# Reordered stages of a fused attention and expert kernel: adjacent cross values, ScalarE prototype norm

## The chip, the core and the metric

The kernel runs on one core of one Trainium2 chip. The metric is device time in microseconds (us) of one execution; lower is better. Runs of one kernel differ by about 0.1% here (1447.82 to 1450.38 us in three).

## What is computed

Four sequences of 1024 rows of 256 numbers, all in fp32, go through two layers. Layer 0 does layer norm, self-attention in windows of 128 rows (16 heads of 16, shifted by 64 rows), top-16 cross-attention to 77 context rows, and a SwiGLU of width 1024, each with a modulation from a condition vector. Layer 1 attends to the same 77 rows as prototypes, routes over three experts, and gates the result. Cut to what matters here:

```
scores = einsum('bqhd,bkhd->bhqk', q, k) / sqrt(D)          # cross-attention, 77 keys
top_s, top_i = top_k(scores, 16);  attn = softmax(top_s)
o = einsum('bhqk,bhqkd->bqhd', attn, take(v, top_i))         # "cross values"
x = x + gate * (o @ w_co + b_co);  x = x + swiglu(ln(x))
nx = layer_norm(x) * gamma + beta                            # layer 1
weights = softmax(nx @ Wq @ (P @ Wk).T / 16);  evidence = weights @ (P @ Wv)
probs = softmax(concat(nx, evidence, anchor) @ router_W + b)
out = x + gate(...) * (sum_e probs_e * expert_e(...) @ out_w + out_b)
```

## The kernel before

The 4096 rows are worked off in 16 units of 256 rows (two tiles of 128), software-pipelined by hand: step k of the function `both` does the self-attention stage for unit a = k + 1, the cross-attention stage for unit c = k, and the MLP and expert stage for unit b = k - 1. After a prologue come 14 steps of `both` (k = 1 to 14), one of `last_cross` (no unit a is left) and one of `last_experts` (unit 15 alone). Each engine has its own copy of these functions with its own order of calls written out, and each engine works strictly in that order. Nothing reorders them at run time; semaphores make one engine wait for another.

All eight PSUM banks are shared by jobs in a fixed order, `BANK_JOBS`. A job's producer on TensorE waits until the previous job of that bank is drained (`wait_free`), and signals `full`; the reader signals `drained`. For the prediction these rows of the table matter: bank 1 holds the self-attention values "v" and then "y01" (turned cross weights of the first tile); bank 2 holds "y02" and then "h00"; bank 4 "mo", then "ln4", then "ps"; bank 5 "m1", "m6", "h01", "h20"; bank 6 "m2", "h10", "e0", "e1"; bank 7 "m7", "wt", "h11", "h21".

The part of a step around the change runs like this:

- TensorE ends the projections of unit a with `a_v` (L826), turns the normalised rows of unit b (`b_turn_normed`, a `turn` of "ln4", four transposes at L776 that read `xnB`), turns the picked cross weights of the first tile (`a_turn_picked(0, s)`, ten transposes at L923 and L930), and multiplies by the prototypes' matrix (`b_proto_scores`, L988, which reads `nxT`). Then come products of the experts' first layer (`b_first_nx`, L1011, eight matmuls each), the turned prototype weights (`b_turn_weights`, L996), the cross values of the first tile (`a_cross_values`, L944 and L950), the evidence products (`b_first_evidence`, L1018), the picked weights of the second tile, the turned inverses of the kept sums (`a_turn_inverses`, L883, reads `kept`), the router (L1003), the cross values of the second tile, and the self-attention scores of unit a (`a_scores`, L844).
- ScalarE copies the values out of bank 1 (`a_copy_values`, writes `va`, L1454), scales the turned rows into `nxT` (`b_affine`, through `modulate`, L1414), copies the turned picks into `probT` (`a_copy_picked`, L1478), takes the exponentials of the prototype scores (`b_proto_exp`, L1554, writes `pw`), then of the second tile's cross scores (`a_cross_exp`, L1499), then copies the turned weights out (`b_copy_weights`, L1560).
- VectorE does the layer norm statistics (`ln_stats`) and their use (`ln_apply`, L2220, writes `xnB`), the top-16 search (`a_topk`, MAX8 and MATCH_REPLACE8 at L2304, L2309 and L2316, the bulk of its work), masks the picked weights (`a_pick`), takes the prototype maxima (`b_proto_shift`, L2351), and normalises the prototype weights (`b_proto_norm`: reciprocal L2357, multiply L2359). The search of the second tile is wrapped around these two. At its end come the kept sums (`a_sum_kept`) and their inverse (`a_invert_kept`, L2285).
- GpSimd computes the inverse deviations (`rstd_of`, L1820 and L1822), subtracts row maxima (`a_shift`, L1835), and spreads the kept inverses (`a_spread`, L1856).

SyncE issues the DMAs (rows of x, results, weights per sequence); the change touches none of them.

Of the kernel before, what the change touches and what calls it, by code (L numbers as in the profile page):

```python
# [147 lines left out]
def bass_pixart_experts(nc, x, cond, ctx_in, w_ada, b_ada, w_qkv, b_qkv, w_so, b_so, w_q, b_q, w_kv, b_kv,  # L148
# [6 lines left out]
    with ExitStack() as stack:  # L155
# [81 lines left out]
        probT = sb("probT", [P, SLOTS, HPS, P])  # L237
        rsum = sb("rsum", [P, TILES, H])
# [350 lines left out]
        def _(pe):  # L589
# [343 lines left out]
            def a_cross_values(t, u):  # L933
# [5 lines left out]
                for e in range(PAR):  # L939
                    wait_drained(pe, f"y{t}{e}", u)  # L940
                    for f, name in enumerate(("xv", "xw")):
                        r = slice(f * MAIN, (f + 1) * MAIN)
                        for s in range(SLOTS):
                            pe.matmul(bank_of(name)[32 * s:32 * s + 32, t * P:(t + 1) * P], vc_main[r, s, 32 * e:32 * e + 32],  # L944
                                      probT[r, e, s, :], start=(e == 0), stop=False, skip_group_check=True)
                wait_drained(pe, f"y{t}2", u)
                for f, name in enumerate(("xv", "xw")):
                    r = slice(f * MAIN, (f + 1) * MAIN)
                    for s in range(SLOTS):
                        last[name] = pe.matmul(bank_of(name)[32 * s:32 * s + 32, t * P:(t + 1) * P], vc_tail[r, s // 2, s % 2, :],  # L950
                                               probT[r, 2, s // 2, :], start=False, stop=True, skip_group_check=True)
# [224 lines left out]
            def both(k, r, batch):  # L1176
# [46 lines left out]
                b_turn_normed(b)  # L1223
# [4 lines left out]
                a_turn_picked(0, 2, c)  # L1228
                if r == 1:
                    pe.wait_ge(readB, batch * 5 + 5)  # L1230
                a_turn_picked(0, 3, c)
                b_proto_scores(b)
                b_first_nx("h00", 0, b)
                b_first_nx("h01", 2 * P, b)
# [4 lines left out]
                if r == 0:  # L1239
                    pe.wait_ge(values_read, batch + 1)  # L1240
                a_cross_values(0, c)
# [7 lines left out]
                b_first_evidence("h10", RH, b)  # L1249
                a_turn_inverses("r2", "xv", c)  # L1250
                b_router(b)
# [38 lines left out]
            def last_cross(c, b):  # L1290
# [21 lines left out]
                b_turn_normed(b)  # L1312
                a_turn_picked(0, 2, c)
                a_turn_picked(0, 3, c)
                b_proto_scores(b)
                b_first_nx("h00", 0, b)
                b_first_nx("h01", 2 * P, b)
                a_cross_values(0, c)
                b_turn_weights(b)
                b_first_nx("h10", RH, b)  # L1320
                b_first_evidence("h00", 0, b)
                b_first_nx("h11", RH + 2 * P, b)
                b_first_evidence("h01", 2 * P, b)
# [4 lines left out]
                b_first_evidence("h10", RH, b)  # L1328
                a_turn_inverses("r2", "xv", c)
                a_cross_values(1, c)  # L1330
                b_first_evidence("h11", RH + 2 * P, b)
                b_router(b)
                a_project("xv", oT2, "co", Wco_g, c)
                b_second(0, (0, 1), b)
                b_first_nx("h20", 2 * RH, b)
                b_second(0, (2, 3), b)
                b_second(1, (0, 1), b)
                b_first_nx("h21", 2 * RH + 2 * P, b)
# [5 lines left out]
                turn("ln3", xnB, c, normed[2], TILES)  # L1344


            def last_experts(b):
# [31 lines left out]
                b_first_evidence("h11", RH + 2 * P, b)  # L1379
                b_second(0, (0, 1), b)  # L1380
                b_first_nx("h20", 2 * RH, b)
                b_second(0, (2, 3), b)
                b_second(1, (0, 1), b)
                b_first_nx("h21", 2 * RH + 2 * P, b)
# [20 lines left out]
        def _(act):  # L1405
# [67 lines left out]
            def a_copy_picked(t, i, u):  # L1473
# [4 lines left out]
                act.activation(probT[:, i, 0:n, :], bank_of(name)[:, 0:n * P].rearrange("p (i q) -> p i q", i=n), ACT.Copy)\  # L1478
# [70 lines left out]
            def b_proto_exp(u):  # L1549
# [6 lines left out]
                i.then_inc(drained[JOB["ps"][0]], 1)  # L1556

# [99 lines left out]
            def both(k, r, batch):  # L1657
# [32 lines left out]
                a_cross_exp(1, 0, c)  # L1690
                b_copy_weights(b)
# [40 lines left out]
            def last_cross(c, b):  # L1732
# [22 lines left out]
                a_copy_picked(0, 2, c)  # L1755
                b_proto_exp(b)
                a_cross_exp(1, 0, c)
                b_copy_weights(b)
                a_cross_exp(1, 1, c)
                a_kept_exp(0, c)  # L1760
# [9 lines left out]
                b_tanh_first("h11", hE[:, 1], 2, 6, b)  # L1770
                b_tanh_first("h20", hE[:, 0], 0, 8, b)
                b_tanh_first("h21", hE[:, 0], 2, 10, b)
                b_tanh_first("hg", gs, 0, 12, b)
                b_modulate(c)

            def last_experts(b):
# [11 lines left out]
                b_proto_exp(b)  # L1788
                b_copy_weights(b)
# [25 lines left out]
        def _(pool):  # L1815
# [146 lines left out]
            def both(k, r, batch):  # L1962
# [11 lines left out]
                a_shift(0, 0, c)  # L1974
                rstd_of(0, EPS0, a)
                wait_full(pool, "ln2", a - 1)
                ln_apply(0, xa, xnA, a)
                a_shift(0, 1, c)
# [22 lines left out]
            def last_cross(c, b):  # L2001
# [14 lines left out]
                a_spread("xv", c)  # L2016
                b_mix_biases(b)
                rstd_of(2, EPS0, c)
# [33 lines left out]
        def _(dve):  # L2052
# [213 lines left out]
            def a_normalise(name, dst, u):  # L2266
# [3 lines left out]
                if name == "xv":  # L2270
                    wait_full(dve, "xw", u)
                    for f, half in enumerate(("xv", "xw")):
# [82 lines left out]
            def b_proto_norm(u):  # L2355
                wait_drained(dve, "ps", u)
                dve.reciprocal(psu[:, :], psu[:, :]).then_inc(proto_steps, 1)  # L2357
                dve.wait_ge(proto_steps, u * 2 + 1)
                dve.tensor_tensor(pw[:, :, :], pw[:, :, :], psu[:, :].rearrange("p (t a) -> p t a", a=1).to_broadcast([P, TILES, LC]),  # L2359
                                  ALU.mult).then_inc(proto_steps, 1)  # L2360
# [168 lines left out]
            def both(k, r, batch):  # L2529

                a, c, b = k + 1, k, k - 1
                ra, xa, xc, xb = (r + 1) % UNITS, xs[(r + 1) % UNITS], xs[r], xs[r - 1]
                b_swiglu(0, b)
# [7 lines left out]
                a_load(ra, batch)  # L2541
                ln_stats(0, xa, a)
# [29 lines left out]
                if r == 1:  # L2572
                    prep_b_evidence(batch, 3, psum[6])
                a_residual(xb, xb, "mo", b)
                wait_drained(dve, "mo", b)
                ln_stats(3, xb, b)
                a_pick(0, 1, c)
# [6 lines left out]
                b_proto_norm(b)  # L2584
# [46 lines left out]
            def last_cross(c, b):  # L2631
# [19 lines left out]
                a_topk("a", 1, 0, c)  # L2651
# [3 lines left out]
                a_pick(0, 1, c)  # L2655
                ln_apply(3, xb, xnB, b)
                a_topk("a", 1, 1, c)
                a_topk("b", 1, 0, c)
                a_topk("a", 1, 2, c)
                b_proto_shift(b)  # L2660
                a_topk("b", 1, 1, c)
                b_proto_norm(b)
# [96 lines left out]
```

## Time and profile before

| | |
|---|---|
| median of 3 runs | 1449.21 us (1447.82 to 1450.38) |
| profiled execution, its own time | 1443.77 us |
| its span, first to last instruction | 1442.0 us |
| instructions | 31061 |
| busy share of the span: TensorE matmul, weight load | 97%, 81% |
| busy share: VectorE, ScalarE, GpSimd | 73%, 58%, 33% |
| mean granted TensorE clock | 0.994 of 2.4 GHz |
| bytes moved | 35 MB, 24 GB/s on average |

The span is measured on the one profiled execution. "Busy" of TensorE counts from the start of a matmul to its modelled end; matmuls overlap, so that the distance between the starts of two neighbours (0.216 us for 256 columns, 0.109 us for a transpose of 128) is what a matmul costs in a stream, not its own length of 0.38 us.

### The profile page before, as it was taken

To read this page: it belongs to the slowest core of one execution; us is meant where nothing else is said; L and a number is where in the kernel's file an instruction comes from. 1 tells how busy PE (TensorE), PEld (TensorE's weight loads), DVE (VectorE), ACT (ScalarE), POOL (GpSimd) and SP (SyncE) were. 2 spreads that over 40 slices of the span, in tenths; PEclk is the share of its full clock that TensorE was granted. 3 is DMA by queue.
4 is the path that set the end of the run, shared out by engine and by line. 5 is a ranking of instruction groups with operands and counts; after the bars stand their busy time and mean duration, and the time that the engine had idled before them with its cause. 6 is when DMAs were issued, how large, how long until landed. Compare 5 with 4: busy or idle time off the path is not lost.

```text
span 1442.0 us, 31061 instructions
## 1 busy us (share of the span) xinstructions
PE 1399.3 (97%) x10145; PEld 1172.1 (81%) x10145; DVE 1050.5 (73%) x4822; ACT 833.3 (58%) x2599; POOL 481.7 (33%) x627
## 2 busy tenths in 40 slices
PE   7989999999999999999999999999999999998997
PEld 5778788888888788888888788888888878887886
DVE  3586869687786868778696786869687786968532
ACT  2473575757566375756647375665757457574423
POOL 1315133333325234332335233233335313332302
PEclk9999999999999999999999999999999999999999
DMA  7510000000010000010010000010010000000000
GB/s 245 202 67 2 1 15 12 9 27 9 19 31 16 1 2 25 2 34 9 19 31 2 15 2 16 11 34 1 9 49 2 16 1 9 1 1 8 2 4 11
DMA packets 27346, 35.06 MB, mean 24 GB/s; under 512 B 3324, under 2 KB 22448, under 8 KB 26929
## 3 DMA queue, kind: packets, MB, share of 16 engines
q1 hardware_dynamic: 27185, 33.07, 7.2%
q8 instruction: 82, 1.34, 0.4%
q14 instruction: 79, 0.65, 0.1%
HBM read 28.83 MB, written 4.22 MB: 23 GB/s over the span
## 4 chain that ended last, share of the span: by engine, by line
PE 80%; DVE 14%; ACT 3%; issue 3%; POOL 1%; SPq 0%; DMA 0%; DVEq 0%; POOLq 0%; ACTq 0%
PE bank L966 12%; PE bank L1011 12%; PE bank L1035 11%; PE bank L1018 6%; PE bank L805 6%; PE bank L975 6%; PE bank L791 5%; DVE knocked L2316 4%; PE bank L854 3%; PE bank L844 2%; PE bank L866 2%; PE bank L923 2%; PE bank L762 2%; PE bank L776 2%; DVE M L2309 2%
## 5 line engine op out<-in xcount | busy, mean ns | idle before, releaser
L966 PE MATMUL bank<-hB,Wm 128*128 128x256 f32 x1024 | 244.3, 385 | 2.2 <-ACT hB L1414 2.2
L966 PEld LDWEIGHTS bank<-hB,Wm 128*128 128x128 f32 x1024 | 191.8, 191 | 33.8 <-issue 7.5
L1011 PE MATMUL bank<-nxT,W1nx 128*128 128x256 f32 x896 | 214.1, 385 | 3.0 <-ACT probT L1478 2.7
L1463 ACT ACTIVATE prob<-bank,rmax 128x128 f32<-128x128 f32 x512 | 179.1, 402 | 29.3 <-DVE rmax L2238 29.3
L1011 PEld LDWEIGHTS bank<-nxT,W1nx 128*128 128x128 f32 x896 | 167.1, 192 | 28.2 <-ACT probT L1478 5.1
L1035 PE MATMUL bank<-W2p,gT 128*128 128x256 f32 x768 | 183.2, 382 | 3.0 <-DVE acc L2395 1.9
L1835 POOL TENSOR_TENSOR scores<-scores,M 128x308 f32<-128x308 f32 x128 | 93.3, 729 | 277.1 <-DVE knocked L2316 275.9
L1035 PEld LDWEIGHTS bank<-W2p,gT 128*128 128x128 f32 x768 | 141.4, 190 | 23.6 <-issue 2.8
L1516 ACT ACTIVATE tbs<-bank,b1half 128x256 f32<-128x256 f32 x128 | 60.5, 473 | 146.4 <-PE bank L966 106.9
L1532 ACT ACTIVATE tbs<-bank,betaH 128x256 f32<-128x256 f32 x224 | 96.3, 497 | 78.4 <-PE bank L1018 78.4
L1820 POOL TENSOR_SCALAR vare<-mv 128x2 f32<-128x2 f32 x64 | 24.9, 388 | 311.8 <-DVE mv L2214 310.5
L1463 ACT ACTIVATION_READ_ACCUMULATOR prob<-bank,rmax 128x1 f32 x512 | 124.2, 243 | 0.0
L975 PE MATMUL bank<-Wm_g,gT 128*128 128x256 f32 x480 | 116.1, 381 | 0.0
L1018 PE MATMUL bank<-wT,Vp 77*128 77x256 f32 x448 | 113.2, 386 | 0.0
L2316 DVE MATCH_REPLACE8 knocked<-M,scores 128x77 f32<-128x77 f32 x512 | 108.4, 223 | 0.2 <-issue 0.2
L2316 DVE MATCH_REPLACE8 knocked<-M,knocked 128x77 f32<-128x77 f32 x512 | 108.3, 222 | 0.2
L975 PEld LDWEIGHTS bank<-Wm_g,gT 128*128 128x128 f32 x480 | 90.3, 190 | 17.0 <-issue 4.2
L2238 DVE TENSOR_REDUCE rmax<-bank 128x4 f32<-128x512 f32 x128 | 80.7, 684 | 21.6 <-PE bank L844 21.6
L1018 PEld LDWEIGHTS bank<-wT,Vp 77*128 77x128 f32 x448 | 80.4, 190 | 14.3 <-issue 5.7
L2304 DVE MAX8 M<-scores 128x8 f32<-128x77 f32 x512 | 83.6, 224 | 0.2
L2309 DVE MAX8 M<-knocked 128x8 f32<-128x77 f32 x512 | 83.1, 223 | 0.0
L2336 DVE SCALAR_TENSOR_TENSOR gT<-tbs,gT 128x256 f32<-128x256 f32 x120 | 51.3, 428 | 37.4 <-ACT gT L1518 37.4
(258 smaller groups left out, 2841.1 us busy)
## 6 DMA issues: line engine op xcount, KB each, us to landing
Wm_g<-in_L_xcond_w_m_dram SPq DMA_DIRECT2D x4, 1024.0 KB, 5.5
W1ev<-in_L_xcond_e_w_dram SPq DMA_DIRECT2D x6, 512.0 KB, 7.3
x<-in_x_dram SPq DMA_DIRECT2D x16, 128.0 KB, 2.4
x<-in_x_dram SPq DMA_DIRECT2D x32, 64.0 KB, 2.3
Wm<-in_L_xcond_w_m_dram SPq DMA_DIRECT2D x1, 2048.0 KB, 8.8
out_dram<-acc SPq DMA_DIRECT2D x16, 128.0 KB, 1.7
out_dram<-acc SPq DMA_DIRECT2D x32, 64.0 KB, 2.0
batch_rows<-row_store SPq DMA_DIRECT2D x4, 384.0 KB, 3.8
```

The source lines that it names most:

```text
L805: m = pe.matmul(bk[:, t * C:(t + 1) * C], src[:, k, t * P:(t + 1) * P], w[:, k, :], start=(opens and k == 0 and t == 0), stop=(k == nk - 1 ...
L966: m = pe.matmul(bank_of(name)[:, half * UT:(half + 1) * UT], Wm1[:, k, c:c + P], hB[:, k, :], start=(k == 0), stop=(k == CB - 1))
L975: m = pe.matmul(bank_of("mo")[:, t * C:(t + 1) * C], gated_of(u)[:, j, t * P:(t + 1) * P], Wm2_g[:, j, :], start=(j == 0 and t == 0), stop ...
L1011: pe.matmul(bank_of(name)[:, n * UT:(n + 1) * UT], W1nx[:, k, c0 + n * P:c0 + (n + 1) * P], nxT[:, k, :], start=(n == 0 and k == 0), stop= ...
L1018: m = pe.matmul(bank_of(name)[:, n * UT:(n + 1) * UT], Vp[:, c0 + n * P:c0 + (n + 1) * P], wT[:, :], start=False, stop=True, skip_group_ch ...
L1035: m = pe.matmul(bank_of(name)[:, t * C:(t + 1) * C], hE[:, e % 2, k, t * P:(t + 1) * P], W2p[:, e * RB + k, :], start=(k == 0 and t == 0), ...
L1463: m = act.activation(prob[:, s, i, :], psum[s][:, i * P:(i + 1) * P], ACT.Exp, bias=rmax[:, t, s * HPS + i:s * HPS + i + 1], accum_out=rsu ...
L1532: act.activation(tb[tb_of(name)][:, n * UT:(n + 1) * UT], bank_of(name)[:, n * UT:(n + 1) * UT], ACT.Tanh, bias=betaH[:, n0 + n:n0 + n + 1 ...
L1835: pool.tensor_tensor(Dx[:, t, g, :], S[:, t, g, :], M12[:, t, g, 0:1].to_broadcast([P, HPS, LC]), ALU.subtract)\
L2304: dve.max(M12[:, t, h, 0:8], S[:, t, h, :]).then_inc(topk, 1)
L2309: dve.max(M12[:, t, h, 8:TOPK], K[:, h, :]).then_inc(topk, 1)
L2316: dve.match_replace(K[:, h, :], top, src, KNOCKED).then_inc(topk, 1)
```

## The change

The turned weights of the first cross tile are copied into `prob` instead of `probT` (`turned_picks`), so that both tiles' turned weights can stand at once, and the two calls of `a_cross_values` follow each other behind `a_turn_inverses`. On TensorE, `b_turn_normed` moves behind all four `a_turn_picked(0, s)`, so that it stands directly ahead of `b_proto_scores`; the products "h01" and "h00" swap; the router moves ahead of the turned inverses. The multiplication of the prototype weights by their inverse sums moves from VectorE (one instruction) to ScalarE (two), behind `a_cross_exp(1, 0)`; only the reciprocal stays on VectorE. VectorE takes the statistics of unit a ahead of `b_swiglu(0)`, and `a_pick(0, 1)` ahead of the MLP's residual. GpSimd does `rstd_of(0)` and `ln_apply(0)` ahead of `a_shift(0, 0)`. In `last_cross` and `last_experts` several blocks change places. The diff, with unchanged lines left out and indentation reduced:

```diff
@@ -235,6 +235,7 @@ buffers
 probT = sb("probT", [P, SLOTS, HPS, P])
+turned_picks = [prob, probT]
 rsum = sb("rsum", [P, TILES, H])
@@ -942,13 +943,13 @@ TensorE, a_cross_values
         pe.matmul(bank_of(name)[32 * s:32 * s + 32, t * P:(t + 1) * P], vc_main[r, s, 32 * e:32 * e + 32],
-        probT[r, e, s, :], start=(e == 0), stop=False, skip_group_check=True)
+        turned_picks[t][r, e, s, :], start=(e == 0), stop=False, skip_group_check=True)
     wait_drained(pe, f"y{t}2", u)
...
         last[name] = pe.matmul(bank_of(name)[32 * s:32 * s + 32, t * P:(t + 1) * P], vc_tail[r, s // 2, s % 2, :],
-        probT[r, 2, s // 2, :], start=False, stop=True, skip_group_check=True)
+        turned_picks[t][r, 2, s // 2, :], start=False, stop=True, skip_group_check=True)
     if t == TILES - 1:
@@ -1220,25 +1221,22 @@ TensorE, both (a = k + 1, c = k, b = k - 1)
     a_v(1, a)
-    b_turn_normed(b)
     if r == 1:
...
     a_turn_picked(0, 2, c)
+    a_turn_picked(0, 3, c)
+    b_turn_normed(b)
     if r == 1:
         pe.wait_ge(readB, batch * 5 + 5)
-    a_turn_picked(0, 3, c)
     b_proto_scores(b)
+    b_first_nx("h01", 2 * P, b)
     b_first_nx("h00", 0, b)
-    b_first_nx("h01", 2 * P, b)
     b_turn_weights(b)
...
     b_first_nx("h10", RH, b)
-    if r == 0:
-        pe.wait_ge(values_read, batch + 1)
-    a_cross_values(0, c)
     b_first_evidence("h00", 0, b)
@@ -1247,8 +1245,11 @@ TensorE, both
     b_first_evidence("h10", RH, b)
+    b_router(b)
     a_turn_inverses("r2", "xv", c)
-    b_router(b)
+    if r == 0:
+        pe.wait_ge(values_read, batch + 1)
+    a_cross_values(0, c)
     a_cross_values(1, c)
@@ -1309,40 +1310,39 @@ TensorE, last_cross
     a_turn_picked(0, 1, c)
-    b_turn_normed(b)
     a_turn_picked(0, 2, c)
     a_turn_picked(0, 3, c)
+    b_turn_normed(b)
     b_proto_scores(b)
+    b_first_nx("h01", 2 * P, b)
     b_first_nx("h00", 0, b)
-    b_first_nx("h01", 2 * P, b)
-    a_cross_values(0, c)
     b_turn_weights(b)
...
     b_first_evidence("h00", 0, b)
+    b_first_evidence("h01", 2 * P, b)
     b_first_nx("h11", RH + 2 * P, b)
-    b_first_evidence("h01", 2 * P, b)
     a_turn_picked(1, 0, c)
...
     b_first_evidence("h10", RH, b)
+    b_router(b)
     a_turn_inverses("r2", "xv", c)
+    a_cross_values(0, c)
     a_cross_values(1, c)
     b_first_evidence("h11", RH + 2 * P, b)
-    b_router(b)
+    b_second(0, (0, 1), b)
     a_project("xv", oT2, "co", Wco_g, c)
-    b_second(0, (0, 1), b)
     b_first_nx("h20", 2 * RH, b)
     b_second(0, (2, 3), b)
+    b_first_nx("h21", 2 * RH + 2 * P, b)
     b_second(1, (0, 1), b)
-    b_first_nx("h21", 2 * RH + 2 * P, b)
+    turn("ln3", xnB, c, normed[2], TILES)
     b_second(1, (2, 3), b)
...
     b_first_evidence("hg", 3 * RH, b)
-    turn("ln3", xnB, c, normed[2], TILES)
-
@@ -1377,11 +1377,11 @@ TensorE, last_experts
     b_first_evidence("h11", RH + 2 * P, b)
+    b_first_nx("h20", 2 * RH, b)
     b_second(0, (0, 1), b)
-    b_first_nx("h20", 2 * RH, b)
     b_second(0, (2, 3), b)
+    b_first_nx("h21", 2 * RH + 2 * P, b)
     b_second(1, (0, 1), b)
-    b_first_nx("h21", 2 * RH + 2 * P, b)
     b_second(1, (2, 3), b)
@@ -1475,7 +1475,7 @@ ScalarE, a_copy_picked
     wait_full(act, name, u)
-    act.activation(probT[:, i, 0:n, :], bank_of(name)[:, 0:n * P].rearrange("p (i q) -> p i q", i=n), ACT.Copy)\
+    act.activation(turned_picks[t][:, i, 0:n, :], bank_of(name)[:, 0:n * P].rearrange("p (i q) -> p i q", i=n), ACT.Copy)\
        .then_inc(drained[JOB[name][0]], 1)
@@ -1554,6 +1554,12 @@ ScalarE, new function
     i.then_inc(drained[JOB["ps"][0]], 1)
+
+def b_proto_norm(u):
+    act.wait_ge(proto_steps, u * 2 + 1)
+    for t in range(TILES):
+        i = act.activation(pw[:, t, :], pw[:, t, :], ACT.Copy, scale=psu[:, t:t + 1])
+    i.then_inc(proto_steps, 1)
@@ -1688,6 +1694,7 @@ ScalarE, both
     a_cross_exp(1, 0, c)
+    b_proto_norm(b)
     b_copy_weights(b)
@@ -1753,11 +1760,12 @@ ScalarE, last_cross
     a_copy_picked(0, 2, c)
+    a_kept_exp(0, c)
     b_proto_exp(b)
     a_cross_exp(1, 0, c)
+    b_proto_norm(b)
     b_copy_weights(b)
     a_cross_exp(1, 1, c)
-    a_kept_exp(0, c)
     b_tanh_first("h00", hE[:, 0], 0, 0, b)
@@ -1768,10 +1776,10 @@ ScalarE, last_cross
     b_tanh_first("h11", hE[:, 1], 2, 6, b)
+    b_modulate(c)
     b_tanh_first("h20", hE[:, 0], 0, 8, b)
...
     b_tanh_first("hg", gs, 0, 12, b)
-    b_modulate(c)
@@ -1786,6 +1794,7 @@ ScalarE, last_experts
     b_proto_exp(b)
+    b_proto_norm(b)
     b_copy_weights(b)
@@ -1971,10 +1980,10 @@ GpSimd, both
     add_bias(1, xc, c)
-    a_shift(0, 0, c)
     rstd_of(0, EPS0, a)
...
     ln_apply(0, xa, xnA, a)
+    a_shift(0, 0, c)
     a_shift(0, 1, c)
@@ -2014,8 +2023,8 @@ GpSimd, last_cross
     a_spread("xv", c)
+    rstd_of(2, EPS0, c)
     b_mix_biases(b)
-    rstd_of(2, EPS0, c)
@@ -2269,7 +2278,7 @@ VectorE, a_normalise
         wait_full(dve, "xw", u)
-        for f, half in enumerate(("xv", "xw")):
+        for f, half in ((1, "xw"), (0, "xv")):
         dve.tensor_tensor(dst[:, f, :], bank_of(half)[:, 0:UT], oT2[:, f, :], ALU.mult).then_inc(drained[JOB[half][0]], 1)
@@ -2352,12 +2361,9 @@ VectorE, b_proto_norm
-def b_proto_norm(u):
+def b_proto_invert(u):
     wait_drained(dve, "ps", u)
     dve.reciprocal(psu[:, :], psu[:, :]).then_inc(proto_steps, 1)
-    dve.wait_ge(proto_steps, u * 2 + 1)
-    dve.tensor_tensor(pw[:, :, :], pw[:, :, :], psu[:, :].rearrange("p (t a) -> p t a", a=1).to_broadcast([P, TILES, LC]),
-        ALU.mult).then_inc(proto_steps, 1)
@@ -2530,6 +2536,8 @@ VectorE, both
     ra, xa, xc, xb = (r + 1) % UNITS, xs[(r + 1) % UNITS], xs[r], xs[r - 1]
+    a_load(ra, batch)
+    ln_stats(0, xa, a)
     b_swiglu(0, b)
@@ -2538,8 +2546,6 @@ VectorE, both
         prep_m(batch)
-    a_load(ra, batch)
-    ln_stats(0, xa, a)
     a_topk("a", 0, 1, c)
@@ -2571,17 +2577,17 @@ VectorE, both
         prep_b_evidence(batch, 3, psum[6])
+    a_pick(0, 1, c)
     a_residual(xb, xb, "mo", b)
...
     ln_stats(3, xb, b)
-    a_pick(0, 1, c)
     a_topk("a", 1, 0, c)
...
     a_topk("a", 1, 2, c)
-    b_proto_norm(b)
+    b_proto_invert(b)
     a_topk("b", 1, 1, c)
@@ -2648,18 +2654,18 @@ VectorE, last_cross
     a_pick(0, 0, c)
-    a_topk("a", 1, 0, c)
+    a_pick(0, 1, c)
     a_residual(xb, xb, "mo", b)
...
     ln_stats(3, xb, b)
-    a_pick(0, 1, c)
+    a_topk("a", 1, 0, c)
     ln_apply(3, xb, xnB, b)
...
     a_topk("b", 1, 0, c)
+    b_proto_shift(b)
     a_topk("a", 1, 2, c)
-    b_proto_shift(b)
+    b_proto_invert(b)
     a_topk("b", 1, 1, c)
-    b_proto_norm(b)
     a_topk("a", 1, 3, c)
@@ -2678,8 +2684,8 @@ VectorE, last_cross
     b_mix(0, b)
+    ln_apply(2, xc, xnB, c)
     b_silu("h11", hE[:, 1], 2, b)
-    ln_apply(2, xc, xnB, c)
     b_mix(1, b)
@@ -2703,7 +2709,7 @@ VectorE, last_experts
     b_proto_shift(b)
-    b_proto_norm(b)
+    b_proto_invert(b)
     b_finish(b - 1, xs[(b - 1) % UNITS])
```

## Rows read from the trace of the kernel before

**Rows 1.** Page, part 1: busy time, share of the span, instructions.

```profile
PE 1399.3 (97%) x10145; PEld 1172.1 (81%) x10145; DVE 1050.5 (73%) x4822; ACT 833.3 (58%) x2599; POOL 481.7 (33%) x627
```

**Rows 2.** Waits: engine, line <- releaser: us in total, times, longest.

```profile
PE bank L923 <- ACT va L1454: 2.7, 10, 0.3
PE bank L1011 <- ACT probT L1478: 2.7, 10, 0.3
...
DVE gT L2336 <- ACT gT L1518: 37.4, 15, 4.7
```

**Rows 3.** Timeline of TensorE, one step: start, us, line, tiles, xcount [idle <- releaser].

```profile
405.63 0.67 PE L776 MATMUL bank<-ident,xnB 128*128 128x128 f32 x4
406.57 1.07 PE L923 MATMUL bank<-ident,picked_first 128*128 128x128 f32 x8 [0.28 <-ACT va L1454]
...
407.69 1.02 PE L988 MATMUL bank<-GpR,nxT 128*128 128x80 f32 x8
408.98 3.72 PE L1011 MATMUL bank<-nxT,W1nx 128*128 128x256 f32 x16 [0.27 <-ACT probT L1478]
...
414.58 0.67 PE L944 MATMUL bank<-probT,vc_main 64*32 64x128 f32 x32
...
415.45 1.99 PE L1018 MATMUL bank<-wT,Vp 77*128 77x256 f32 x8
...
421.03 0.66 PE L883 MATMUL bank<-ident,kept 128*128 128x128 f32 x4
421.53 0.51 PE L1003 MATMUL bank<-Vp,wT 77*128 77x3 f32 x4
...
424.04 0.50 PE L844 MATMUL bank<-km,qT 32*128 32x256 f32 x4
```

**Rows 4.** Timeline of ScalarE, same step.

```profile
405.83 0.60 ACT L1454 ACTIVATE va<-bank 128x512 f32<-128x512 f32 x1 [0.79 <-PE bank L826]
406.34 1.02 ACT L1414 ACTIVATE nxT<-bank,cols 128x256 f32<-128x256 f32 x2
```

**Rows 5.** Timeline of VectorE, same step.

```profile
408.75 0.32 DVE L2351 TENSOR_REDUCE pm<-bank 128x2 f32<-128x154 f32 x1 [0.16 <-PE bank L988]
...
410.44 0.16 DVE L2357 RECIPROCAL psu<-psu 128x2 f32<-128x2 f32 x1
410.63 0.85 DVE L2359 TENSOR_TENSOR pw<-pw,psu 128x154 f32<-128x154 f32 x1
```

**Rows 6.** Timeline of GpSimd, same step.

```profile
420.01 0.97 POOL L1856 COPY kept<-kinv 128x256 f32<-128x256 f32 x2 [2.97 <-DVE kinv L2285]
```

**Rows 7.** Source view of L2359: duration ns min/median/max.

```profile
L2359 DVE TENSOR_TENSOR pw<-pw,psu x16: 320/852/854, 163.2 to 1402.9; 128x154 f32<-128x154 f32 x16
```

**Rows 8.** Timeline of TensorE, another step (the one where `xnB` is latest).

```profile
322.07 0.38 PE L826 MATMUL bank<-Wqkv,hA 128*128 128x256 f32 x1
...
326.03 0.48 PE L1011 MATMUL bank<-nxT,W1nx 128*128 128x256 f32 x1
```

**Rows 9.** Timeline of TensorE in the last two steps.

```profile
1329.99 1.31 PE L776 MATMUL bank<-ident,xnB 128*128 128x128 f32 x4 [4.47 <-DVE xnB L2220]
...
1334.26 5.54 PE L1011 MATMUL bank<-nxT,W1nx 128*128 128x256 f32 x16
...
1358.88 2.00 PE L1035 MATMUL bank<-W2p,gT 128*128 128x256 f32 x8 [0.97 <-DVE acc L2395]
...
1371.28 3.34 PE L966 MATMUL bank<-hB,Wm 128*128 128x256 f32 x9 [2.19 <-ACT hB L1414]
...
1411.41 1.11 PE L1018 MATMUL bank<-wT,Vp 77*128 77x256 f32 x4
1413.54 2.00 PE L1035 MATMUL bank<-W2p,gT 128*128 128x256 f32 x8 [1.02 <-ACT gT L1539]
```

**Rows 10.** Windows: us, busy of five engines, PEclk (granted clock), DMA share, GB/s.

```profile
97.00:99.00 2.00, 0.90 (x7) 0.42 (x5) 2.00 (x5) 2.00 (x13) 0.00 (x0) 1.00 0.01 4
...
1372.00:1376.00 4.00, 4.00 (x12) 3.18 (x12) 0.80 (x2) 0.84 (x2) 0.00 (x0) 0.57 0.00 0
```

## The prediction

> **What bounds the kernel now.** I read the page first: TensorE is busy 97% of the span and no other engine passes 73% [rows 1]. So only two things can move the time: work that TensorE is spared, and gaps in its stream. Then the waits of TensorE by releaser: the two that this change aims at in every step are the turned picks waiting for ScalarE's `va` and the product "h00" waiting for ScalarE's copy of the picks [rows 2]. Then the timelines of one step, engine by engine [rows 3 to 6]. I count from T = 405.63, when the last projection has passed and the turned rows of "ln4" start. There the reader sees TensorE's order and where it pauses: ln4 at T, picks at T + 0.94, prototype scores at T + 2.06, "h00" at T + 3.35, first cross values at T + 8.95, turned inverses at T + 15.40, attention scores at T + 18.41 [rows 3]. I looked at all 14 steps; 10 have these times within 0.1 us, the other four have `xnB` later, and the latest of them starts "h00" at T + 3.74 (326.03 less 322.07 + 0.22) [rows 8].
>
> **The change in a step of `both`, part by part.**
>
> *Turned rows behind the picks.* The picks need bank 1 free, that is `va` copied. The copy ends at T + 0.80 and TensorE goes on 0.14 later [rows 3, 4]. It starts only when the values are full, so nothing in the change makes it earlier. Today ln4's four transposes (0.44) fill half of that pause. In the new order nothing does: picks still start at T + 0.94 and end where the prototype scores start today, T + 2.06. The four transposes follow, to T + 2.50. ScalarE must now turn them into `nxT` while TensorE has nothing else in its order: its two activations took 1.02 us [rows 4], start 0.2 behind the transposes (they start at T + 0.71, with the turned rows begun at T and two of them held a little for `xnB`) and release TensorE 0.14 later: 2.50 + 0.2 + 1.02 + 0.14 = T + 3.86. Today ten transposes of picks hide exactly this. Eight products of 0.112 take 0.9, so "h01" starts at T + 4.76 instead of "h00" at T + 3.35: **1.4 us later**. The swap of h01 and h00 takes away the wait of 0.27 for "y02" [rows 3], already counted in this. Bounds: if ScalarE's scaling were all hidden it would be 0.2, if more of its queue stood ahead 1.8; ScalarE's order shows `b_affine` first in line, so I keep 1.4. In the step where `xnB` is latest it is 1.0.
>
> *Cross values together.* The block of 48 small matmuls takes 0.87 to the next group (414.58 to 415.45) [rows 3], of which a part is the change of tile shape before and behind it. One such change on each side goes: between 0 and 0.3, I take 0.2. No wait of its own is added: ScalarE has the first tile's copies long before.
>
> *Norm on ScalarE.* VectorE loses the multiply, 0.85 of 16 in 14 cases, 0.32 in two [rows 5, 7]. In each of the 14 a GpSimd subtraction starts 0.02 earlier and ends within it, in the other two none runs. I take 0.85 off VectorE, at least 0.32. The Trainium skill, page "SBUF — State Buffer", section "Who interferes with whom", says that a VectorE instruction with two SBUF inputs is held by a GpSimd instruction that reads SBUF and starts first, and by it the whole 0.85 goes. The two copies of 77 columns on ScalarE cost between nothing and 1.0 us (a 256-column activation of `nxT` is about 0.5). They are covered: TensorE asks for the weights 3.46 after "h01", at T + 8.2, and they are there at about T + 7.8. That cover is thin; gone, each 0.1 shows.
>
> *What this does to VectorE.* `b_proto_shift` now waits for the late scores, with the search of the second tile queued behind it. It starts 1.06 behind the first product (408.75 less 407.69) [rows 3, 5], so at T + 4.92 instead of T + 3.12, 1.8 later; 0.85 comes back from the multiply, so the rest of the chain (search, picks, kept sums, GpSimd's spread that ends at T + 15.35 [rows 6]) is 0.95 later: T + 16.3. The 0.98 us that the statistics of unit a save by moving into VectorE's idle stretch ahead of `b_swiglu(0)` (37.4 us in 15 steps, 2.5 each [rows 2]) pay for `a_pick(0, 1)` ahead of the residual, and leave `xnB` no later; they can't pull the search past a wait that now stands in the middle of it. GpSimd's reordering costs nothing: its subtractions are needed several us later. No DMA moves.
>
> *TensorE meets it.* It comes to the turned inverses at 4.76 + (15.40 - 3.35) - 0.87 + 0.43 (router ahead, 421.53 to 421.96 in step with the second cross values) - 0.1 = T + 16.3, together with the spread. From there to the attention scores it needed 3.01 (421.03 to 424.04); now without the router and with both cross calls 3.01 - 0.43 + 0.87 - 0.2 = 3.25. Scores start at T + 19.55 instead of T + 18.41: 1.14 per step. I find no idle time of TensorE further on that could take this back. 14 steps, less 0.4 for the step with late `xnB`: **+15.6 us**. Bounds per step: 0.9 (both shape changes and the present pause before the inverses gone) to 1.7 (multiply only worth 0.32): 12.6 to 23.8.
>
> **The last two steps.** Here TensorE does wait [rows 9], and the change works:
> - `last_cross`, 4.47 idle for `xnB`: VectorE gets there at most 0.6 earlier, and picks are out of the way, but the pause for `nxT` now shows. I take -0.5, between 0 and everything: the idle time, with the low clock behind it (16 products in 5.54 against 3.72 [rows 3, 9]), is 8.0.
> - The second expert's products, 0.97 idle (1.13 between starts), in both steps alike: "h21" now fills it, -2.3.
> - First MLP product of unit 15, 2.19 idle (2.35 between starts) for `hB`: turned and modulated earlier, all gone. The granted clock behind it is 0.57 of full for 4 us [rows 10], so it returns 4 x 0.43 = 1.7 too: -4.05.
> - 1.02 idle (1.18 between starts) before the first expert in `last_experts`, "h20" fills it: -1.2.
>
> Sum -8.05. **Net +15.6 - 8.0 = +7.6 us**, against the profiled execution's own 1443.77 us: 1451.4. That execution is 5.4 below the median of the runs shown; I keep this distance: 1449.2 + 7.6 = **1456.8 us**.
>
> **Rivals.**
> - *The clock falls in each step.* Two pauses of 0.94 and 1.36 us now stand 1.6 us apart. In the trace a stretch with TensorE busy 0.90 of 2.00 us kept its clock (1.00), the wait of 2.19 lost it (0.57) [rows 9, 10]. If the new pair counts as the latter, each step loses up to 1.7 more: 14 x 1.7 = 24, 1480 us. For it: the pair lies between the two. Against: every pause alone is short. The Trainium skill, page "TensorE: Matmul & The Clock Gate", section "HAM oscillation — how this bites in real kernels", describes waits that recur in every pass of a loop and leave the clock halved behind each; by that the sum would be this rival's. Chance 0.10.
> - *The end returns more than the steps cost* (other side). In the last two steps the whole idle time goes, first wait and its low clock included: 8.0 + 7.55 = 15.5, and each step costs its lower bound 0.9, 12.6 in all: -2.9, 1446.3 us. It decides once a step costs under 0.9 and the first wait is gone. For it: the waits are there. Against: VectorE's own work sets the 4.47, and it stays. Chance 0.12.
> - *VectorE's chain, not TensorE, sets the step,* and TensorE's lateness is absorbed: if the scaling of `nxT` finds cover and `b_proto_shift` comes only 0.85 later, the inverses stay at T + 15.4 and a step costs the 0.24 by which the tail behind them is longer, up to 0.6: +3.4 to 8, less 8: 1444.6 to 1449, most of it within 0.2%. Against: TensorE would have to be at the inverses 0.9 earlier than I count. Chance 0.11.
> - *It does nothing*: the pauses only change place, 1449 us. Chance 0.03.
>
> **How the numbers follow.** The forecast has 0.64, nearly all of it slower by over 0.2% (2.9 us, about what a measurement of this kernel can tell from no change). Slower 0.62 + 0.10 = 0.72; within 0.2% 0.02 + 0.11 + 0.03 = 0.16; faster 0.12. The forecast's own bounds are 1449.2 + 12.6 - 8.05 = 1453.8 and 1449.2 + 23.8 - 7.55 = 1465.5. The range reaches down to 1445 to take in the two lower rivals, and up to 1474 for a clock that falls in half of the steps.
>
> **What would show it.** In the changed trace: picks of the first tile at T + 0.94, now with 0.8 to 0.9 idle for `va`; 1.2 to 1.4 idle ahead of the prototype scores, released by ScalarE's `nxT`, 14 times; no wait at the first L1011; VectorE idle 1.5 us or more ahead of L2351; granted clock near 1.00 there. In the last step no wait of 2.19 for `hB`. I am wrong if the wait for `nxT` is under 0.6 us, if the step grows by less than 0.6 or over 1.7, or if the last two steps shrink by less than 5 or more than 12 us.

## The result and the profile after

The changed kernel takes 1455.25 us (median of 5 runs, 1450.72 to 1455.92) against 1449.21 us before: ratio 1.0035, 95% interval [1.0019, 1.0052], 6.0 us slower. The prediction said 1456.8 us, +7.6. All runs of the kernel before in this study lie between 1443.5 and 1450.4 us, a wider spread than the 0.1% of its first three.

The page of the profiled execution (its own time 1454.47 us), parts 1 and 2, answers to [rows 1]:

```profile
span 1452.7 us, 31076 instructions
PE 1394.5 (96%) x10145; PEld 1168.8 (80%) x10145; DVE 1036.5 (71%) x4806; ACT 844.3 (58%) x2631; POOL 475.8 (33%) x627
PEclk9999999999999999999999999999999999999999
```

TensorE does the same 10145 matmuls and is busy 5 us less, in a span 10.7 us longer: what grew is idle time. The waits of TensorE (us in total, times, longest), as in [rows 2]:

```profile
PE bank L989 <- ACT nxT L1414: 18.0, 15, 1.2
PE bank L924 <- ACT va L1454: 10.9, 14, 0.8
...
PE bank L777 <- DVE xnB L2229: 3.6, 4, 2.9
```

A wait that was not in the list before, for `nxT`, comes in each of the 14 steps and once in `last_cross`, and is 1.2 us long. The wait for `va` went from 2.7 to 10.9. The wait for ScalarE's copy ahead of "h00" is gone, and so are those of the last steps for `hB` and for the expert's sums. The timeline of one step on TensorE, from T = 411.87, answers to [rows 3]:

```profile
412.81 1.06 PE L924 MATMUL bank<-ident,picked_first 128*128 128x128 f32 x8 [0.78 <-ACT va L1454]
413.72 0.38 PE L931 MATMUL bank<-ident,picked_first 128*128 128x128 f32 x2
413.94 0.60 PE L777 MATMUL bank<-ident,xnB 128*128 128x128 f32 x4
415.74 1.09 PE L989 MATMUL bank<-GpR,nxT 128*128 128x80 f32 x8 [1.20 <-ACT nxT L1414]
416.66 3.66 PE L1012 MATMUL bank<-nxT,W1nx 128*128 128x256 f32 x16
...
428.31 0.63 PE L884 MATMUL bank<-ident,kept 128*128 128x128 f32 x4
428.88 0.67 PE L945 MATMUL bank<-prob,vc_main 64*32 64x128 f32 x32
...
429.56 0.69 PE L945 MATMUL bank<-probT,vc_main 64*32 64x128 f32 x32
...
431.46 0.91 PE L845 MATMUL bank<-km,qT 32*128 32x256 f32 x9
```

Picks at T + 0.94, prototype scores at T + 3.87, first products at T + 4.79, inverses at T + 16.44, attention scores at T + 19.59. ScalarE in the same step, answering to [rows 4]:

```profile
412.07 0.60 ACT L1454 ACTIVATE va<-bank 128x512 f32<-128x512 f32 x1 [0.79 <-PE bank L827]
414.57 1.02 ACT L1414 ACTIVATE nxT<-bank,cols 128x256 f32<-128x256 f32 x2 [1.90 <-PE bank L777]
415.49 1.36 ACT L1478 ACTIVATE prob<-bank 128x512 f32<-128x512 f32 x3
...
418.75 0.61 ACT L1561 ACTIVATE pw<-pw,psu 128x77 f32<-128x77 f32 x2
```

ScalarE idles 1.90 us and then does the scaling for which TensorE stands. The norm on ScalarE takes 0.61 and is done at T + 7.49, 0.8 ahead of TensorE's turn of the weights. VectorE waits 2.28 us for the prototype scores:

```profile
416.86 0.32 DVE L2360 TENSOR_REDUCE pm<-bank 128x2 f32<-128x154 f32 x1 [2.28 <-PE bank L989]
```

**Where the time went.** I cut each profiled execution in three: up to T of the first step of `both` (T1), from there to T of the fourteenth, and from there to the end.

| kernel | to T1 | 13 periods | T14 to the end | T1 to the end |
|---|---|---|---|---|
| before | 158.2 | 1091.2 | 192.6 | 1283.8 |
| after | 161.8 | 1105.1 | 185.9 | 1290.9 |

T is the start of the last projection matmul of `a_v` plus 0.216. Within a trace most steps have the same times from T on to 0.02 us (the inverses of search_ahead stand at T + 16.32 in all 14); the part ahead of T1 does not: over the twelve kernels of this study it takes 158.1 to 162.8 us though nearly nothing there differs. So the traces say +7.1 for what the change touches. The medians say +6.0, with an interval of 2.8 to 7.5 us that holds 7.1. The 10.7 between the two profiled executions is these 7.1 and 3.6 of the start.

### The profile page after: what moved, and what is told of

It reads as the page before. It is cut to its first block, busy times and chain, and to the rows that moved or that the text cites. A ratio compares the mean times of both kernels' runs of the same rounds, so it can differ in the third digit from the quotient of the medians.

```text
span 1452.7 us, 31076 instructions
## 1 busy us (share of the span) xinstructions
PE 1394.5 (96%) x10145; PEld 1168.8 (80%) x10145; DVE 1036.5 (71%) x4806; ACT 844.3 (58%) x2631; POOL 475.8 (33%) x627
## 4 chain that ended last, share of the span: by engine, by line
PE 88%; DVE 7%; ACT 3%; issue 1%; SPq 0%; POOL 0%; DMA 0%; DVEq 0%; POOLq 0%; ACTq 0%
PE bank L967 15%; PE bank L1012 12%; PE bank L1036 11%; PE bank L976 7%; PE bank L1019 7%; PE bank L806 6%; PE bank L792 6%; PE bank L855 3%; PE bank L845 2%; PE bank L924 2%; PE bank L777 2%; PE bank L867 2%; PE bank L827 2%; DVE knocked L2325 2%; PE bank L763 2%; PE bank L911 1%
## 5 line engine op out<-in xcount | busy, mean ns | idle before, releaser
L1036 PE MATMUL bank<-W2p,gT 128*128 128x256 f32 x768 | 182.6, 381 | 1.0 <-ACT gT L1539 1.0
L1829 POOL TENSOR_SCALAR vare<-mv 128x2 f32<-128x2 f32 x64 | 17.8, 278 | 367.5 <-DVE mv L2223 366.1
L2354 DVE SCALAR_TENSOR_TENSOR gT<-tbs,gT 128x512 f32<-128x512 f32 x96 | 70.7, 749 | 7.6 <-ACT gT L1539 7.6
```

Source lines behind the costliest of these rows:

```text
L1036: m = pe.matmul(bank_of(name)[:, t * C:(t + 1) * C], hE[:, e % 2, k, t * P:(t + 1) * P], W2p[:, e * RB + k, :], start=(k == 0 and t == 0), ...
```

## The experiments

All were built from the changed kernel unless it says otherwise. Each line of `both` named here stands in all 14 steps. Ratios are against the kernel before on the same chip (medians 1446.70, 1449.58 and 1446.85 us on the three chips used). The differences in us are of "T1 to the end" in one trace of each kernel, because runs of one kernel spread by 3 to 8 us. Where such a difference is small, the paragraph behind the table at the end of this section says how much of it is the clock.

**ln4_back.** TensorE's turned rows ahead of the picks again:

```diff
     a_v(1, a)
+    b_turn_normed(b)
...
     a_turn_picked(0, 3, c)
-    b_turn_normed(b)
```

> The changed kernel with one thing undone: in the 14 steps of both, the turned rows (ln4) stand ahead of the picks again. Theory P (TensorE's uncovered wait for nxT and for va is the loss): picks stay at T+0.94, prototype scores go from T+3.86 to about T+2.06, the attention scores from T+19.59 to about T+17.9, so 1.7 us per step and 24 us in all: about 1431 us, below both kernels. Rival V (VectorE's search, queued behind the late prototype maxima, sets the step): the same move also brings the maxima 1.8 earlier, so this run alone gives the same sign; search_ahead tells the two apart. Rival C (the adjacent cross values or the norm on ScalarE cost something themselves): the step stays longer than T+18.4 and the kernel lands at 1441 or above.

1425.96 us, ratio 0.9852 [0.9825, 0.9878]; T1 to the end 1264.3, 26.7 less than after and 19.5 less than before. TensorE, T = 406.63:

```profile
406.63 0.60 PE L777 MATMUL bank<-ident,xnB 128*128 128x128 f32 x4
407.57 1.06 PE L924 MATMUL bank<-ident,picked_first 128*128 128x128 f32 x8 [0.34 <-ACT va L1454]
...
408.69 1.02 PE L989 MATMUL bank<-GpR,nxT 128*128 128x80 f32 x8
409.54 3.66 PE L1012 MATMUL bank<-nxT,W1nx 128*128 128x256 f32 x16
...
421.20 0.64 PE L884 MATMUL bank<-ident,kept 128*128 128x128 f32 x4
...
424.35 0.93 PE L845 MATMUL bank<-km,qT 32*128 32x256 f32 x12
```

Scores of the prototypes at T + 2.06 with no wait ahead of them, attention scores at T + 17.72. One block of four transposes in the wrong place turned a gain of 19.5 us into a loss of 7.1. Rival C, a cost of the other parts, falls. In this run VectorE's chain moved too, as the expectation says, so it does not tell TensorE's lateness from VectorE's.

**search_ahead.** VectorE's search fills the wait ahead of the prototype maxima:

```diff
-    b_proto_shift(b)
     a_topk("a", 1, 2, c)
-    b_proto_invert(b)
+    b_proto_shift(b)
     a_topk("b", 1, 1, c)
+    b_proto_invert(b)
```

> The changed kernel with VectorE's order altered in both: the search a(1,2) ahead of the prototype maxima and b(1,1) ahead of the reciprocal, so that VectorE's idle 2.2 us ahead of the maxima hold a search of 1.4 us. Theory P: TensorE is what comes last, nothing changes, 1455 us within 0.2%, turned inverses still at T+16.44. Rival V: the inverses come up to 0.9 us earlier per step, up to 12 us in all, 1443 us.

1452.19 us, 1.0030 [1.0015, 1.0046]; T1 to the end 2.8 less than after. The inverses (L884) came at T + 16.32 instead of T + 16.44, T = 408.88:

```profile
425.20 0.64 PE L884 MATMUL bank<-ident,kept 128*128 128x128 f32 x4
...
428.35 1.15 PE L845 MATMUL bank<-km,qT 32*128 32x256 f32 x16
```

With VectorE's chain out of the way TensorE's own order still needs until T + 16.32, so its lateness alone makes nearly all of the loss; V is worth 0.12 at this point (0.26 to 0.31 in four of the 14 steps) and 2.8 us in all, not 12. P's "nothing" was a little too strict. The medians can't tell this kernel from the changed one (1.0030 and 1.0035). GpSimd's spread of the kept inverses, which ends VectorE's chain, shows how near the two paths lie; after, and in search_ahead:

```profile
427.22 0.97 POOL L1865 COPY kept<-kinv 128x256 f32<-128x256 f32 x2 [2.96 <-DVE kinv L2294]
...
422.83 0.97 POOL L1865 COPY kept<-kinv 128x256 f32<-128x256 f32 x2 [2.96 <-DVE kinv L2294]
```

It ends at T + 16.32 in the changed kernel and at T + 14.92 here. In the changed kernel both paths thus reach the inverses at the same time, and freeing VectorE's alone gives back almost nothing. That freeing TensorE's alone would give as little is read from the end of the spread and was not tried.

**ln4_alone.** The kernel before, with only this move (the reverse of the diff of ln4_back):

> The kernel before with only the move of the turned rows behind the picks, in the 14 steps of both. Theory P: prototype scores from T+2.06 to T+3.86; h00, which here still waits for ScalarE's copy of y02 behind nxT, from T+3.35 to about T+5.0; with VectorE's multiply still in place the inverses come at T+17.2 and the attention scores at T+20.2 instead of T+18.4: 1.8 per step, +25 us, about 1474 us. Theory N (the move is harmless and the loss of the change lies in another part): within 0.2% of 1449 us.

1471.94 us, 1.0167 [1.0145, 1.0189]; T1 to the end 26.4 more than before. Prototype scores at T + 3.86, "h00" at T + 5.02, inverses at T + 17.27, attention scores at T + 20.27 in the step of T = 412.11. Without the other parts the move costs 26 us, 22.9 of them in the 13 periods; theory N falls. About 1.5 of the 26.4 stand in `last_experts`, whose order is alike in both kernels: the granted clock was halved there for 3.4 us more.

**ends_alone.** `both` as before on all engines, the multiply on VectorE, `last_cross` and `last_experts` as changed:

```diff
 # both: the kernel before's, on TensorE, ScalarE, GpSimd, VectorE
-    b_proto_norm(b)          # ScalarE, last_cross and last_experts
 # VectorE, b_proto_invert: the multiply again
+    dve.wait_ge(proto_steps, u * 2 + 1)
+    dve.tensor_tensor(pw, pw, psu broadcast, ALU.mult).then_inc(proto_steps, 1)
```

> The changed orders of last_cross and last_experts alone: both is as in the kernel before on every engine, and the multiply of the prototype norm stays on VectorE everywhere. If the end returns what the prediction counted, the steps of both are as before (scores at T+18.41) and the rest from the last step's T to the end is 8 us shorter: 1441 us. Rival: the multiply on ScalarE carried part of the gain of the end, then 1 to 2 us less.

1435.72 us, 0.9918 [0.9892, 0.9944]. T14 to the end is 184.7, 7.9 less than before: the count of 8.0 holds without ScalarE's norm, and the rival falls. But the 13 periods were 2.3 shorter too, with attention scores at T + 18.25, not T + 18.41. That is something which the prediction had not priced; xv_first takes it up.

**norm_on_vector.** ln4_back with the multiply on VectorE (the second half of the diff above, and no `b_proto_norm` on ScalarE):

> The kernel ln4_back with the multiply of the prototype norm on VectorE again, everywhere. With the turned rows early, TensorE reaches the inverses at about T+14.7 and VectorE's chain becomes the last: the multiply puts 0.85 us into it, the inverses come at T+15.4 and the attention scores at about T+18.5 instead of T+17.9: 0.6 per step, 9 us more than ln4_back. Rival: only the 0.32 us that the multiply takes alone count, 4 us; or TensorE still comes last and nothing changes.

1439.64 us, 0.9942 [0.9924, 0.9959]; 12.9 more than ln4_back. TensorE now waits for VectorE ahead of the second tile's picks; T = 405.57:

```profile
417.92 0.66 PE L924 MATMUL bank<-ident,scores 128*128 128x128 f32 x4 [0.37 <-DVE scores L2335]
418.79 0.66 PE L924 MATMUL bank<-ident,scores 128*128 128x128 f32 x4 [0.22 <-DVE scores L2335]
```

Such waits come 28 times here, and in ln4_back none. Inverses at T + 15.47 against T + 14.57: 0.90 per step, more than the 0.6 expected. The expectation took TensorE for the last at this point, but in ln4_back VectorE's chain already was: the spread of the kept inverses ends at T + 14.44 there and the inverses follow 0.13 later, against T + 15.35 and 0.12 here. So the whole multiply counts. The multiply lasted 0.85 us in 15 of 16 steps and 0.32 in one.

**norm_alone.** The kernel before with only the multiply on ScalarE:

> The kernel before with only the multiply of the prototype norm moved to ScalarE. norm_on_vector showed it worth 0.9 us per step where VectorE's chain came last. In the kernel before TensorE and the chain reach the inverses within about 0.1 us of each other in ten of 14 steps: theory P expects 0 to 0.1 per step there and 0.2 to 0.5 in the four steps with late xnB, 1 to 3 us less in all. Rival V (VectorE's chain sets the step of the kernel before as well): 0.85 per step, 12 us less.

1441.35 us, 0.9960 [0.9947, 0.9974]; 5.4 less than before: 3.9 in the periods, 1.5 at the end. Of these 1.5 some 0.9 are the clock: the first 16 products of `last_cross` took 4.59 us from start to start instead of 5.47. V's 12 is refuted; P's 1 to 3 was too low. The inverses came at T + 15.33 in 12 of 14 steps, against 15.39 to 16.18 before, 0.18 on average and 2.5 us in all. The other 1.4 of the periods stand behind the inverses: 0.7 between them and the last evidence product (2.50 us instead of 2.55 per step), 0.5 ahead of the first attention score and 0.3 behind it; why was not tried. In the 13 periods the same edit is thus worth 3.9 us in the old order and 11.6 (1092.3 less 1080.7) in ln4_back.

**cross_apart.** ln4_back with the first tile's cross values at their old place:

```diff
     b_first_nx("h10", RH, b)
+    a_cross_values(0, c)
...
     a_turn_inverses("r2", "xv", c)
-    a_cross_values(0, c)
     a_cross_values(1, c)
```

> The kernel ln4_back with the first tile's cross values back at their old place behind the products h10, in both. The change of tile shape is then paid twice: 0.2 to 0.3 us more per step, 3 to 4 us in all, if TensorE comes last. Rival: the block at its old place fills time in which TensorE would wait for the kept inverses, then nothing changes or it gets faster.

1431.09 us, 0.9877 [0.9847, 0.9907]; 3.6 more than ln4_back, 0.24 per period on average and 0.28 in most steps. Adjacent calls spare that much.

**xv_first.** ln4_back with one line of `a_normalise` as before:

```diff
-    for f, half in ((1, "xw"), (0, "xv")):
+    for f, half in enumerate(("xv", "xw")):
```

> The kernel ln4_back with one line of a_normalise as before: VectorE multiplies the half in bank 4 (xv) ahead of the half in bank 0 (xw). The prediction gave this line no price at all. In the trace the distance from the last evidence product to the first attention score fell from 0.46 us to 0.31 us with the change. If the order of the two halves does it (bank 0 is what the first score waits for), the distance goes back to 0.46: 0.15 per step, 2 us in all over ln4_back. Rival: it comes from the separate buffer of the picks or from the place of the cross values, then it stays 0.31 and nothing changes.

1427.64 us, 0.9871 [0.9847, 0.9894]; 2.7 more than ln4_back, and the distance to the first attention score is back at 0.46 us in 11 of 14 steps (0.31 in 13 of 14 with the line). In the trace of before the last evidence product of the step starts at 423.58 and the first score at 424.04. The line does it: the scores' first bank is that of "xw" (bank 0 in `BANK_JOBS`). In the 13 periods it is worth 2.3 us.

**stats_back.** ln4_back with the old places of statistics and picks:

```diff
 # VectorE
-    a_load(ra, batch); ln_stats(0, xa, a)     # ahead of b_swiglu(0)
+    a_load(ra, batch); ln_stats(0, xa, a)     # ahead of a_topk("a", 0, 1)
-    a_pick(0, 1, c)                           # ahead of a_residual
+    a_pick(0, 1, c)                           # behind ln_stats(3)
 # GpSimd: a_shift(0, 0, c) ahead of rstd_of(0) again
```

> The kernel ln4_back with the orders of statistics, pick(0,1) and shift(0,0) of the kernel before on VectorE and GpSimd, in both. The prediction priced this part at nothing: within 0.2% of ln4_back, with up to 0.4 us more in the step where xnB is latest. Rival: with the turned rows ahead of the picks, xnB is asked for at T and comes up to 0.9 us late in four of 14 steps: 1 to 2 us more.

1428.63 us, 0.9872 [0.9843, 0.9900]; 2.0 more than ln4_back. The rival was right: TensorE waits for `xnB` 8 times and 4.4 us instead of 4 times and 3.6. But only 1.2 of the 2.0 us stand in the 13 periods. The other 0.8 stand in `last_cross`, which is the same in both kernels, where the halved clock met the first 16 products at another moment; stats_back and ln4_back:

```profile
1323.18 6.12 PE L1012 MATMUL bank<-nxT,W1nx 128*128 128x256 f32 x16
...
1325.98 5.03 PE L1012 MATMUL bank<-nxT,W1nx 128*128 128x256 f32 x16
```

The medians can't tell the two kernels apart.

**values_first.** ln4_back, with values ahead of queries:

```diff
 # TensorE
-    a_q(a)
     a_v(0, a)
     a_v(1, a)
+    a_q(a)
 # ScalarE
-    a_scale_queries(a)
     a_copy_values(a)
     b_affine(b)
+    a_scale_queries(a)
```

> The kernel ln4_back with the projection of the values ahead of that of the queries on TensorE, and on ScalarE the copy of the values and the scaling of nxT ahead of the queries, in both. The picks then have no wait for va (0.5 us at T+0.44), and the prototype scores start when nxT is ready, about T+1.9 instead of T+2.06. TensorE's order is what comes last: 0.2 us less per step, 2 to 3 us in all. Rival: with VectorE's chain last, only the start of the prototype maxima counts, the same 0.2. Rival: ScalarE's queries come later and delay something behind them: no gain.

1425.78 us, 0.9853 [0.9830, 0.9877]; counted from the end of the last projection as elsewhere, T1 to the end is 1261.5, 2.8 less than ln4_back. No wait for `va` is left in TensorE's list. About 0.8 of the 2.8 are again the clock in `last_cross` (16 products in 4.57 us), so that the order gives about 2.0, 1.8 of it in the periods. By the medians it is level with ln4_back.

All traces together (us; values_first with its T shifted by the 1.73 of the queries' products):

| kernel | median | 13 periods | T14 to the end | T1 to the end |
|---|---|---|---|---|
| ln4_back | 1425.96 | 1080.7 | 183.6 | 1264.3 |
| search_ahead | 1452.19 | 1102.6 | 185.6 | 1288.2 |
| ln4_alone | 1471.94 | 1114.1 | 196.1 | 1310.2 |
| ends_alone | 1435.72 | 1088.9 | 184.7 | 1273.7 |
| norm_on_vector | 1439.64 | 1092.3 | 184.9 | 1277.2 |
| norm_alone | 1441.35 | 1087.3 | 191.1 | 1278.5 |
| cross_apart | 1431.09 | 1083.8 | 184.0 | 1267.8 |
| xv_first | 1427.64 | 1083.0 | 184.0 | 1266.9 |
| stats_back | 1428.63 | 1081.9 | 184.4 | 1266.3 |
| values_first | 1425.78 | 1078.9 | 182.6 | 1261.5 |

One stretch of "T14 to the end" does not repeat. In the changed kernel and in all kernels built from it, `last_cross` and `last_experts` have the same order on TensorE. What follows the first 16 products of `last_cross` takes 95.3 to 95.4 us in each of them (95.7 in ends_alone). From the first pick to the end of these products it takes 12.6 (values_first) to 14.1 us (stats_back), with the granted clock halved for part of it, and 13.3 in ln4_back. Differences to ln4_back in the last column therefore carry up to 0.8 us of clock either way. Without this stretch they are 26.3 for the changed kernel, 12.7 for norm_on_vector, 3.4 for cross_apart, 2.4 for xv_first, 1.2 for stats_back and -2.0 for values_first.

## Why the prediction was right, by its own steps

- *Turned rows behind the picks.* Predicted: prototype scores at T + 3.86, "h01" at T + 4.76, 1.4 us late. Measured: 3.87 and 4.79. The reading that nothing hides ScalarE's scaling any more was the whole case; ln4_back and ln4_alone show it from both sides (26.7 and 26.4 us; 24.4 and 22.9 in the 13 periods).
- *Cross values together.* Taken as 0.2 per step in its own paragraph, but as 0.1 ahead of the inverses and 0.2 behind them in the sum; measured 0.24 on average and 0.28 in most steps (cross_apart).
- *Norm on ScalarE.* Weights were to be there at T + 7.8 and were at T + 7.49. The 0.85 is right as what VectorE is spared, since undoing it costs 0.90. The Trainium skill's rule on the shared read interface ("SBUF — State Buffer", section "Who interferes with whom") agrees with this case: 0.85 where a GpSimd subtraction ran beside the multiply, 0.32 where none did.
- *VectorE and TensorE meet at the inverses.* Predicted T + 16.3 for both. TensorE's own order gets there at T + 16.32 (search_ahead) and the spread ends at T + 16.32, so both counts were right. The transposes follow the spread 0.12 later, at T + 16.44; this hand-over the sum had left out.
- *A step in all.* Predicted +1.14, measured +1.18 in the step shown. The mean over the 13 periods is 1.07: the four steps in which `xnB` was late lose less (0.6 to 1.0), because the picks now cover that lateness. The prediction allowed this for one of them. The ninth step, which the prediction counts among its ten alike, lost only 0.65: its attention scores already started at T + 18.76 before. All 14 steps cost about 15.1 us, predicted +15.6.
- *The one term that was missing* is the order of the two halves in `a_normalise`. The diff has it, the prediction gave it no price, and it returns 0.15 per step, some 2.4 us in all (xv_first). That the sum of the step came out within 0.04 us all the same is luck: against the 0.15 stands that the inverses came 0.14 later than counted.
- *The statistics ahead* were priced at nothing. They are worth about 1.2 us in ln4_back; in the changed kernel itself this was not tried.
- *The last two steps.* Predicted -8.05; measured 185.9 - 192.6 = -6.7, in which one step's +1.2 stands, so -7.9. The total is right partly by luck. The clock behind the wait for `hB` (32 products in 7.12 us instead of 8.86) and the waits that the experts' products were to fill returned what was counted. But from the first pick of `last_cross` to its first product it took 1.1 us less, not 0.5, a wait that the prediction did not have took 1.2 back, and the wait for `xnB` in `last_experts` fell from 0.57 to 0.25. The timelines of the changed kernel's last steps, answering to [rows 9]:

```profile
1347.82 0.41 PE L777 MATMUL bank<-ident,xnB 128*128 128x128 f32 x2 [2.93 <-DVE xnB L2229]
...
1350.09 1.97 PE L989 MATMUL bank<-GpR,nxT 128*128 128x80 f32 x8 [1.21 <-ACT nxT L1414]
...
1369.60 1.99 PE L1036 MATMUL bank<-W2p,gT 128*128 128x256 f32 x8 [1.02 <-ACT gT L1539]
...
1380.06 0.60 PE L777 MATMUL bank<-ident,xnB 128*128 128x128 f32 x4
...
1386.55 5.83 PE L967 MATMUL bank<-hB,Wm 128*128 128x256 f32 x26
```

The first wait split in two, 2.93 for `xnB` and 1.21 for `nxT`; a new one of 1.02 came at 1369.60, where the first expert's products now stand ahead of the output projection; and unit 15's first MLP product starts with no wait at full speed (26 in 5.83 us, where 9 took 3.34 [rows 9]).

- *The rivals.* The clock did not fall in the steps, so this rival falls. The waits in every pass of a loop that the Trainium skill's page "TensorE: Matmul & The Clock Gate" describes ("HAM oscillation — how this bites in real kernels") last about 3 to 5 us there. The pauses here are 0.94 and 1.36 us, so that page did not speak for the rival as the prediction has it, and no step here tests it. Windows of the changed kernel, with the granted clock in the third column from the right, answering to [rows 10]:

```profile
411.87:415.90 4.03, 2.05 (x17) 1.71 (x16) 2.71 (x24) 1.92 (x4) 0.70 (x1) 1.00 0.01 3
...
1348.00:1352.00 4.00, 2.58 (x13) 2.14 (x12) 3.17 (x25) 2.58 (x6) 0.94 (x2) 0.63 0.00 0
1352.00:1356.00 4.00, 4.00 (x11) 3.19 (x11) 3.91 (x33) 1.94 (x7) 0.70 (x1) 0.52 0.02 6
```

  "The end returns more than the steps cost" failed on both its conditions: the steps cost 1.07, and most of the first wait stayed. "VectorE's chain sets the step" is refuted: TensorE's own order alone needs until T + 16.32 (search_ahead), not T + 15.4. "It does nothing" falls with the 7.1 us of the traces.

## What to carry to other kernels

A reordering that removes waits of 0.3 us can uncover a latency that nothing in the list of waits shows, because it was hidden completely: before moving a producer next to its consumer, add up what stands between the two today and what the reader in the middle takes (here 1.36 us from the last transpose to the first product). Then ask of each engine at the meeting point who comes last; the same instruction taken off VectorE was worth 3.9 us of the 13 periods in one order and 11.6 in the other. If two engines come to it together, speeding up one of them shows nothing. And price every line of the diff: one swapped loop was worth over 2 us.

## What the runs showed of the hardware

- TensorE kept its full granted clock with two pauses of 0.94 and 1.36 us, 1.6 us apart, in all 14 steps (busy 2.05 of 4.03 us, clock 1.00), and lost it in the last-but-one step behind waits of 2.93 and 1.21 us (0.63, then 0.52; these are means of windows in which it was partly at 2.4 and partly at 1.2 GHz).
- The spread of the start is the clock as well. From 20 to 40 us the granted clock was 1.00 in the profile of before and of stats_back (T1 = 158.2 both) and 0.83 in those of after (161.8) and norm_alone (162.8). In all twelve profiles T1 goes with it: 158.1 to 158.2 in the five with a clock of 1.00 there, 159.7 to 162.8 in the other seven. What decides it was not tried.

```profile
20.00:40.00 20.00, 20.00 (x144) 13.96 (x146) 9.63 (x28) 11.14 (x43) 0.93 (x2) 1.00 0.65 202
```

  for before, and for after:

```profile
20.00:40.00 20.00, 20.00 (x119) 14.06 (x118) 7.92 (x24) 9.11 (x40) 0.93 (x2) 0.83 0.65 204
```
